# A three-layer graph network on one core: layer 3's dense products beside the first 12 of 18 gathered slots

## What is computed

```
src, dst = edges plus one self loop per node
dinv = rsqrt(degree)
h = x                                   # [6250, 256] f32
for W, b in ((W1, b1), (W2, b2), (W3, b3)):     # 256 -> 512 -> 512 -> 256
    h = h @ W
    msg = h[src] * dinv[src] * dinv[dst]
    h = relu(segment_sum(msg, dst) + b)
out = layernorm(x + h)                  # over the 256 features
```

## Time and profile before

| | us |
|---|---|
| median of 3 runs | 2979.7 (2963.2 to 2984.22) |
| the profiled execution | 2971.93 |
| its span, first to last instruction | 2970.2 |
| PE busy | 2388.2 (80% of the span) |
| POOL busy | 1696.7 (57%) |
| DVE busy | 994.1 (33%) |
| ACT busy | 718.8 (24%) |
| line 1727 into ps_T and ps_h, busy | 215.7 and 207.1 |
| line 1728 into ps_T and ps_h, busy | 178.5 and 174.3 |
| mean granted clock of PE | 0.902 |

### The profile page before, as it was taken

The page is one execution under the profiler, slowest core; times in us unless marked ns, Lnnn a source line. Parts: engine busy times, 40 slices in busy tenths (PEclk is TensorE's granted clock), DMA queues, the critical chain, the costliest instruction groups (busy, mean ns, idle before and its releaser), DMA issues.

```text
span 2970.2 us, 39333 instructions
## 1 busy us (share of the span) xinstructions
PE 2388.2 (80%) x12137; PEld 1629.3 (55%) x12138; DVE 994.1 (33%) x1126; ACT 718.8 (24%) x1501; POOL 1696.7 (57%) x1768
## 2 busy tenths in 40 slices
PE   7866687778687788779788888788888789988897
PEld 6754465555555666334333334333343378888887
DVE  8775222122122221234233323333331223323232
ACT  7411122222121221112121222212221123333332
POOL 4366555555455554666666666666666655555553
PEclk9787899889898999989899989889999989999999
DMA  5445554444454554667767666766767666666663
GB/s 180 137 131 170 160 163 143 145 147 142 126 161 144 153 153 141 197 211 226 221 210 225 208 217 212 224 213 211 225 211 255 186 186 187 191 184 184 181 189 97
DMA packets 219981, 537.93 MB, mean 181 GB/s; under 512 B 38444, under 2 KB 88483, under 8 KB 219827
## 3 DMA queue, kind: packets, MB, share of 16 engines
q0 software_dynamic: 117216, 365.08, 42.2%
q1 hardware_dynamic: 83955, 123.53, 12.0%
q10 hardware_dynamic: 18656, 47.20, 5.0%
HBM read 448.05 MB, written 87.61 MB: 180 GB/s over the span
## 4 chain that ended last, share of the span: by engine, by line
PE 51%; another core or an unknown queue 20%; issue 15%; DVE 6%; ACT 4%; ACTq 1%; DVEq 1%; POOL 1%; DMA 1%; SPq 0%; POOLq 0%
PE ps_acc L1640 9%; PE ps_d L1640 9%; PE ps_o L1689 6%; PE ps_acc L1636 5%; PE ps_d L1739 4%; PE ps_T L1727 3%; PE ps_T L1728 3%; PE ps_h L1727 2%; PE ps_h L1728 2%; PE ps_h L1680 2%; PE ps_l L1710 2%; PE ps_d L1594 1%; ACT big L1404 1%; PE ps_e L1710 1%
## 5 line engine op out<-in xcount | busy, mean ns | idle before, releaser
L727 POOL DMA_INDIRECT rows<-table,idx x1249 | 1200.6, 961 | 768.5 <-issue 369.9
L949 DVE SCALAR_TENSOR_TENSOR sel<-ps_e,firsts,dstT 128x1152 f32<-128x1152 f32 (+1 forms) x214 | 303.2, 1417 | 1200.9 <-PE ps_acc L1640 313.9
L1640 PE MATMUL ps_acc<-rows,sel 128*128 128x512 f32 (+2 forms) x1496 | 632.7, 543 | 76.7 <-DVE acc L1029 37.5
L727 POOL DMA_INDIRECT rows<-table_parts,idx x483 | 456.4, 945 | 395.4 <-PE ps_acc L1636 168.0
L1640 PE MATMUL ps_d<-rows,sel 128*128 128x512 f32 (+2 forms) x1190 | 526.6, 557 | 19.4 <-issue 12.0
L1640 PEld LDWEIGHTS ps_acc<-rows,sel 128*128 128x128 f32 x1496 | 281.2, 210 | 218.3 <-issue 183.5
L1689 PE MATMUL ps_o<-low,hT 128*128 128x512 f32 (+1 forms) x784 | 293.0, 519 | 66.7 <-ACT hT L1347 49.1
L1636 PE MATMUL ps_acc<-rows,sel 128*128 128x256 bf16 (+1 forms) x1533 | 257.2, 287 | 55.8 <-DVE acc L1029 34.1
L1640 PEld LDWEIGHTS ps_d<-rows,sel 128*128 128x128 f32 x1190 | 209.7, 198 | 149.5 <-issue 133.3
L1689 PEld LDWEIGHTS ps_o<-low,hT 128*128 128x128 f32 x784 | 154.6, 202 | 187.8 <-issue 118.7
L1739 PE MATMUL ps_d<-big 128*128 128x256 bf16 x1470 | 241.6, 284 | 8.4 <-issue 8.4
(11 more groups left out here) (190 smaller groups left out, 2340.5 us busy)
## 6 DMA issues: line engine op xcount, KB each, us to landing
built<-big SPq DMA_DIRECT2D x84, 384.0 KB
low<-built ACTq DMA_DIRECT2D x84, 384.0 KB
rows<-table,idx POOLq DMA_INDIRECT x1249
table<-made SPq DMA_DIRECT2D x49, 256.0 KB
acc<-table SPq DMA_DIRECT2D x49, 256.0 KB
built<-big SPq DMA_DIRECT2D x28, 416.0 KB
low<-built ACTq DMA_DIRECT2D x28, 416.0 KB
table_parts<-big SPq DMA_DIRECT2D x24, 384.0 KB
```

Of the source, the lines that this page charges most:

```text
L727: pool.indirect_dma_start(out=to, out_offset=None, in_=its[0:nodes, :], in_offset=bass.IndirectOffsetOnAxis(ap=idx[:, of, k:k + 1], axis=0 ...
L949: v.scalar_tensor_tensor(to[:, k:k + FRONT, :], numbers.unsqueeze(1).broadcast_to([P, FRONT, P]), firsts[:, bass.ds(t, 1)], dstT[:, bass.d ...
L1640: return mm(to[:, 0:w], sel[:, k, :], rows_of[phase][:, k, 0:w] if first is None else first, start=start, stop=stop)
```

## The change

A constant `DENSE_BESIDE = 12` is new, and the share of units of a slot is worked out from it in place of SLOTS = 18. With it the 196 units of a group stand beside the 3 x 12 first slots of its windows, 5.44 at a slot in place of 3.63, and none stands beside the last six slots of a window.

```diff
-    GROUP, DENSE_OF = 3, 4
+    GROUP, DENSE_OF, DENSE_BESIDE = 3, 4, 12
...
                     def beside(k):
-                        u = SLOTS * b + ORDER.index(k)
-                        n = SLOTS * GROUP
-                        for at in range(u * DENSE_OF * T // n, (u + 1) * DENSE_OF * T // n):
+                        u, until = (DENSE_BESIDE * b + min(ORDER.index(k) + i, DENSE_BESIDE) for i in range(2))
+                        n = DENSE_BESIDE * GROUP
+                        for at in range(u * DENSE_OF * T // n, until * DENSE_OF * T // n):
                             d, h = divmod(at, T)
                             dense(g, d, h, first)
```

## The result

The changed kernel is slower: 3026.0 us (median of 4 runs, 3015.0 to 3028.7) against 2982.0 us for the kernel before on the same chip (4 runs, 2963.2 to 2988.9), a ratio of 1.016 with a 95% interval of 1.013 to 1.019. The forecast was 3050 us, 3012 to 3088. The profiled execution took 3015.0 us (span 3013.3), 43 us more than that of the kernel before.

The account below looks back on a forecast made before the run. PE was taken to set layer 3's pace, losing its idle time at dense products; waits of 63 us plus 25 for the clock less 12 for vanished gaps gave 76 us on 2971.9, 3048, stated as 3050 us, range 3012 to 3088.

Parts of the forecast that it names:

- The five waits: PE in layer 3 waits for ACT's widening at pieces 1, 7, 10, 12 and 15: 63.1 us more in all.
- piece 10: Window 1, behind slot 8: PE's 2.41 us against a chain of 5.10, a 2.69 us wait seven times, 18.8 us.
- piece 15: Window 2, behind slot 8: PE's 1.03 us against a chain of 5.10, a 4.07 us wait, 28.5 us in all.
- piece 7: Window 1, behind slot 0: 4.51 us against 5.08 for the chain, a 0.57 us wait in seven groups, 4.0 us.
- piece 12: Window 2, behind slot 0: an existing wait grows by 0.90 us, 6.3 us in all.
- other idle times: PE's gaps in layer 3 without a profiled cause, about 35 us: some fall into the new waits, 12 us less.
- The clock: PE drops to half rate behind the waits at pieces 15, 10 and 1: 25 us, with bounds of 12 and 34.
- likeliest case: Layer 3's waits and half clock, less vanished gaps, cost 76 us, 3050 us in all; chance 0.55.
- rival "shorter": Gaps without a cause go and the clock falls only at piece 15: 40 us, 3012 us; chance 0.22.
- rival "faster": Six slots in a row end PE's gaps and half clocks, at most 52 us gained: -36 us, 2936 us; chance 0.04.
- chains behind slot 8: DVE's sel and dense tile, then ACT's square root and widening, hold pieces 10 and 15 until 5.10 us after slot 8: 47.3 us.
- Late releases: PE's releases can come some 5 us late and lengthen the chains at slot 8: nothing put down, up to 20 us in range.

Follow-up runs that it names:

- e1: Changed kernel with ACT's square roots of dense tiles 1 and 2 moved behind pieces 10 and 15: 2964.2 us, ratio 0.994 to the kernel before.
- e2: Changed kernel with DVE finishing dense tiles 1 and 2 ahead of the first half of the next sel: 2970.1 us, 0.993 of the kernel before.
- e5: Kernel before (units beside all 18 slots) with six kinds of square root one piece later on ACT: 2458.1 us, 0.992 of the kernel before.
- e8: ACT's program as in the kernel before, units beside the last 9 slots of a window: 2457.2 us, 0.991 of the kernel before.
- e4: Changed kernel with 17 useless products on PE ahead of the wait for piece 15: 3015.2 us, 1.011 of the kernel before.
- e3: Changed kernel with units beside the first 15 slots in place of 12: 2965.2 us, 0.995 of the kernel before.
- e9: The kernel before, unchanged, profiled on a quicker chip: 2479.4 us, ratio 1.000.
- e10: The changed kernel, unchanged, on the quicker kind of chip: 2555.9 us, 1.030 of the kernel before.

## Why the prediction was right, point by point

- **Where the loss is: right.** The five waits, at the five pieces, each behind a square root and a widening, are in the timeline of the changed kernel; e1 and e2 take two of them away by breaking the chain at either end, and e5 to e8 all five. PE does not wait at line 1640.
- **The size of the waits: right to some hundredths of a us.** With the tail (0.16 us by which the last product ends later than the next one would have started), piece 10 costs 2.67 us (2.69 worked out), piece 15 4.05 (4.07), piece 7 0.58 (0.57), piece 12 grew by 0.89 (0.90). The formula of 0.238 us a unit and 0.43 a slot held at 15 slots too (0.23 against 0.24).
- **How often: one wrong.** Piece 15 waits in six groups and not seven. The last group has no next window, so DVE has no `sel` to make at slot 8 there, and the square root hangs on nothing. That is 4 us of the 28.5. At piece 10 the kernel before had 2.7 us of small waits already, which the prediction had counted among its other idle times. The named waits together grew by 54.6 us, or 57 with the tails (33 gaps in place of 17), against 63.1.
- **The clock: right in size.** PE's work at 1.2 GHz grew from 34.6 to 80.9 us, 46.3 us, half of which is 23 us more work; 25 was the estimate. The split was about right as well: the lower level stands behind piece 15 in all six, behind piece 10 in five of seven, behind piece 1 in five of six (one of six before). The Trainium skill (TensorE: Matmul & The Clock Gate, HAM oscillation) has every burst behind a wait start cold in a kernel that waits some 3 to 5 us each time; the prediction read this as a rule for every wait, and its upper bound of 34 us did not come. The trace agrees with the page for the waits of 3.89 us. The shorter ones went either way: on the quicker chip the same wait of 2.51 us at piece 10 brought the lower clock in one of seven.
- **The other idle times: the term that was mis-sized.** The prediction took 12 us off for gaps that vanish into the new waits. They fell from 40.7 to 22.3 us, by 18.4. Each of them also has a tail of 0.16 us, which the profile counts as busy time, and there are 26 in place of 58, so 5.1 us more went with them: some 23.5 us where 12 were put down. With that the sum is 54.6 + 2.6 + 23.1 - 18.4 - 5.1 = 56.8 us, against the 53.8 by which layer 3 grew from its first dense product to PE's last; 3 us stay open. Of the 22 us between the forecast sum of 76 and the 53.8, this term has 11.5, the waits 6 and the clock 2.
- **The time.** By the medians the kernel lost 44 us, by the two profiled executions 43, of which layer 3 has +53.8 and the unchanged stages ahead of it -10.7. Which of the two is typical, 44 or 54, one profile of each kernel can't tell: in e1 to e4 as well the difference of layer 3 from this one profile of the kernel before is 6 to 15 us higher than that of the medians (e1: -11 against -19), so its layer 3 was probably some 10 us shorter than usual. 3026 lies between the likeliest case (3050) and the rival "shorter" (3012), a little nearer to the latter. Half of that rival came true: the gaps without a cause went, but the clock fell behind pieces 1 and 10 as well, not only behind piece 15. A group took 88.5 and 90.5 us where 92 was said, the clock of layer 3 is 0.93 (0.94), and layer 3 is above the 590 us under which the reading would have been wrong.
- **The reason for that term: wrong.** The gaps do not vanish into the waits. e1 has none of the two large waits and as few other gaps (21.2 us). They go with the order on PE: 21 to 25 us in the four profiles on this kind of chip with six slots in a row, 29.0 with three (e3), 40.7 with none. These are single executions, and why it is so was not tested. It is half of the rival "faster", whose gain exists on this kind of chip, with some 24 us where up to 52 were allowed, and which does not decide since the chains behind slot 8 bind. It was rightly put at a small chance, but its gain and the main loss do not exclude each other, and should have been added.
- **Late releases: no part.** The prediction allowed up to 20 us for chains that start late. Some of PE's releases of a piece do come late on this chip (see the last section), but of the thirteen waits behind slot 8 twelve are within 0.3 us of their usual 2.51 or 3.89 us, and one is 3.36.

## What to carry to other kernels

When work is moved on one engine, list the instructions on it that start a chain on other engines and those that wait for one, and count what stands between the two of each pair before and after: here that count, times two prices from the timeline, gave every new wait to a few hundredths of a us. An instruction that waits for another engine, in a program of fixed order, holds what stands behind it: put it behind the last item that somebody needs soon (the square roots one piece later were worth 0.8% for the kernel before, e5 on the quicker kind of chip). And a term for idle time that has no cause in the profile should be priced apart from the waits, since it follows the chip: the same change cost 1.6% on one and 3.0% on another.

## What the runs showed of the hardware

**Two kinds of chip.** The kernel before takes 2983 us on one and 2479 to 2481 us on three others. The waits of 2.51 and 3.89 us are the same on both kinds. What differs ahead of layer 3 is PE's idle time, 513 us on the first and 200 us on a quicker one (profiled executions, stretches of 2386 and 1956 us), and its busy time, 1874 against 1755 us, at a granted clock of 0.89 against 0.95. In layer 3 the other gaps are 40.7 against 8.3 us. Why the chips differ no run shows.

**Some of PE's releases come late on the first kind alone.** The same place as the earlier trace rows, the end of piece 6 in group 1, in e9, the timeline of the kernel before on a quicker chip:

```profile
2062.00 0.28 PE L1728 MATMUL ps_h<-pairs_r,rows_r 128*128 128x256 f32 x1
...
2062.39 1.59 ACT L1422 ACTIVATE rows_r<-low 128x1664 fp32r<-128x1664 bf16 x1 [1.09 <-PE ps_h L1728]
```

ACT starts 0.11 us after the product ends; in the earlier trace rows it was 4.91 us. How many releases are late is harder to say, since the traces of the first chip lack many records of semaphore updates: 17,554 stand in that of the kernel before, 43,056 in that of the same kernel in e9. Of the 112 releases of a piece in layer 3, 62 have no recorded update within 0.3 us of the product's end on the first chip. In 46 of these ACT stood idle and started within 0.3 us of the late record, which came 2.9 us after the product on the mean and 8.7 at most, so these are late in fact. In 10 ACT had started before the record, so there the record is missing and the release was not that late. On the quicker chips no record is later than 0.01 us. That late releases and gaps come and go together speaks for one origin, but what it is no run here shows. For the same reason "issue" in a profile of the first chip does not say that PE waited for nothing.

**The clock after a short wait.** In the 4 us behind a wait of 3.89 us PE's clock was at 1.2 GHz for 2.8 to 4.0 us, in all twelve cases (six each in the changed kernel and in e10). Behind shorter waits it went either way, and the length doesn't sort them: of the 2.51 us waits at piece 10 one of seven in e10 was followed by the lower level, of the waits of 1.83 to 1.92 us at piece 1 three of four in e9 and none of two in the kernel before. Behind 3.84 us filled with useless products it stayed at 2.4 GHz in all six.
